# Graph layer on one core: the edge stage rebuilt around a broadcast row of relative targets, with W2 applied at the end

## What is computed

```python
h = maximum(layernorm(x), 0)
e = concatenate([h[src], h[dst]], axis=1)          # 200000 x 128
m = relu(e @ W1 + b1) @ W2 + b2                    # 200000 x 64
s = segment_sum(m, dst); cnt = segment_sum(1, dst)
out = x + s / maximum(cnt, 1)[:, None]
```

## Time and profile before

| what | value |
|---|---|
| median of 3 runs without a profile | 2057.42 us |
| profiled execution: first to last instruction | 3104.2 us |
| busy in it: PE / DVE / ACT / POOL | 1916.4 / 866.9 / 884.8 / 1516.6 us |
| indirect DMAs, mean busy of one | 1563, 944 ns |
| HBM traffic | 149 MB, 48 GB/s over the profiled span |
| mean granted TensorE clock | 0.748 |

### The profile page before, as it was taken

One profiled execution on the slowest core, in us unless ns is written; L12 is line 12 of the kernel. 1 busy time (PEld: TensorE's weight loads), 2 busy tenths in 40 slices (PEclk: granted clock), 3 DMA queues, 4 the chain that ended last, 5 costly groups with the idle time before them and its releaser, 6 DMA issues.

```text
span 3104.2 us, 46493 instructions
## 1 busy us (share of the span) xinstructions
PE 1916.4 (62%) x11540; PEld 1632.1 (53%) x11541; DVE 866.9 (28%) x2889; ACT 884.8 (29%) x2458; POOL 1516.6 (49%) x1611
## 2 busy tenths in 40 slices
PE   6256555655655566765556665565655667665568
PEld 6255444545555555554445555454555556554457
DVE  6122222222222222222222222222222222222224
ACT  3123222322222222222222222222222222222224
POOL 5445444544545444454445444454545445454451
PEclk9577777777777776677777667777777766677778
DMA  6311111111111111111111111111111111111111
GB/s 183 92 52 46 43 44 43 43 43 44 44 43 45 43 43 43 44 45 43 44 43 46 43 44 43 43 45 44 44 44 44 44 43 44 44 44 44 44 44 43
DMA packets 112927, 150.93 MB, mean 49 GB/s; under 512 B 32653, under 2 KB 83212, under 8 KB 112750
## 3 DMA queue, kind: packets, MB, share of 16 engines
q0 software_dynamic: 50016, 102.53, 12.6%
q1 hardware_dynamic: 62170, 46.62, 5.1%
q10 hardware_dynamic: 564, 0.23, 0.0%
HBM read 133.09 MB, written 16.07 MB: 48 GB/s over the span
## 4 chain that ended last, share of the span: by engine, by line
another core or an unknown queue 41%; PE 28%; issue 14%; ACT 10%; DVE 4%; DVEq 2%; DMA 1%; ACTq 1%; SPq 0%; POOL 0%; PEldq 0%; POOLq 0%
PE bank L874 12%; PE bank L885 11%; ACT spread L490 4%; ACT member L514 3%; PE bank L894 2%; DVE z L685 2%; ACT spans_i L497 1%; DVEq L689 1%; PE bank L975 1%; PE bank L817 1%; ACT idx L484 1%; PE bank L905 1%; PE bank L899 0%; PE bank L906 0%
## 5 line engine op out<-in xcount | busy, mean ns | idle before, releaser
L388 POOL DMA_INDIRECT g<-p_table,idx x1563 | 1476.0, 944 | 1504.6 <-ACT idx L484 1022.8
L874 PE MATMUL bank<-qw,spread 128*128 128x128 f32 x3126 | 647.1, 371 | 1044.4 <-ACT spread L490 985.2
L874 PEld LDWEIGHTS bank<-qw,spread 128*128 128x128 f32 x3126 | 551.4, 265 | 1106.8 <-ACT spread L490 857.0
L490 ACT CAST spread<-bank 128x512 f32<-128x512 bf16 x391 | 228.7, 585 | 1713.2 <-remote 1335.2
L885 PE MATMUL bank<-member,r 128*128 128x128 f32 x3126 | 616.9, 360 | 63.3 <-DVE acc L704 42.5
L697 DVE TENSOR_TENSOR area<-area,spans_i 1x128 f32 x391 | 109.6, 280 | 1949.0 <-ACT spans_i L497 1773.9
L885 PEld LDWEIGHTS bank<-member,r 128*128 128x128 f32 x3126 | 544.8, 263 | 106.6 <-DVE acc L704 38.9
L675 DVE TENSOR_SCALAR member<-columns,rel_e 128x128 f32<-128x128 f32 x1563 | 349.2, 290 | 107.0 <-PE bank L885 85.2
L508 ACT ACTIVATE r<-z 128x512 f32<-128x512 f32 x391 | 246.1, 630 | 371.5 <-DVE z L685 279.5
L685 DVE TENSOR_TENSOR z<-bank,g 128x512 f32<-128x512 f32 x391 | 263.7, 674 | 0.0
L514 ACT CAST member<-member 128x512 bf16<-128x512 f32 x391 | 235.3, 602 | 4.3 <-DVE member L675 4.3
(11 more groups left out here) (66 smaller groups left out, 434.8 us busy)
## 6 DMA issues: line engine op xcount, KB each, us to landing
qw<-q_table SPq DMA_DIRECT2D x391, 64.0 KB
g<-p_table,idx POOLq DMA_INDIRECT x1563
p_table<-area SPq DMA_DIRECT2D x10, 560.0 KB
q_table<-area SPq DMA_DIRECT2D x10, 560.0 KB
xs<-in_x_dram SPq DMA_DIRECT2D x5, 560.0 KB
out_dram<-xs SPq DMA_DIRECT2D x3, 672.0 KB
acc<-in_src_dram SPq DMA_DIRECT2D x1, 768.0 KB
acc<-in_dst_dram SPq DMA_DIRECT2D x1, 768.0 KB
```

The costliest lines, as they stand in the source:

```text
L388: nc.gpsimd.indirect_dma_start(out=g[:, k, j * HID:(j + 1) * HID], out_offset=None, in_=p_table, in_offset=bass.IndirectOffsetOnAxis(ap=id ...
L490: nc.scalar.copy(spread[:, k % 2, :, :].rearrange("p c e -> p (c e)")[:, 0:w], t_bank[k % 2][:, 0:w]).then_inc(spread_done, 1)
L874: last = nc.tensor.matmul(z_bank[k % 2][:, HID * j:HID * (j + 1)], spread[:, k % 2, j, :], qw[:, k, :], start=True, stop=True)
```

## The change

What it does, engine by engine:
- **W2 at the end.** `acc` holds sums of the 128 hidden values. The two multiplies per quad (lines 905, 906) and the copies before them go. At the end each of the 100 transposes becomes two fp32 matmuls into 64 columns: `acc` (125 strided columns as weights) by W2, and `count` (one partition, 125 strided columns as weights) by b2.
- **Spread.** At the start VectorE makes `rel_q` (bf16, four instructions of 128 x 512). Per quad TensorE broadcasts one row of it to 128 partitions (one bf16 matmul of 512 columns) and VectorE compares it with the partition's number, from PSUM, into `spread`. The transposes, the bf16 copy of member and the copy of spread go.
- **Member** is one instruction of 128 x 512 for a quad in place of four of 128 x 128, with two tensor inputs in SBUF. The counts read its upper halves as bf16.
- **Sum and relu in place** in the slot of the gather; a slot is free after the sum, in a ring of 16 instead of 12. Windows of q have a ring of 8.
- **GpSimd** gathers with indices straight from `src_e`, the first 16 quads without a wait of the edge stage. All engines' loops are unrolled, with waits on constants.
- ScalarE keeps one instruction per quad, the relu.

```diff
-RING = 12
+RING = 16
+WINDOWS = 8
@@ gpsimd
-            def gather(n, k, use):
-                ready = pool.to_reg(n + 1)
-                pool.wait_ge(p_out[0], all_out[0])
-                pool.wait_ge(idx_ready, ready)
+            pool.wait_ge(src_table, QT)
+            def gather(n):
+                k = n % RING
+                if n >= RING:
+                    pool.wait_ge(u_psum, n - RING + 1)
                 for j in range(chunks_of(n)):
                     nc.gpsimd.indirect_dma_start(
...
@@ scalar
+                for n in range(QUADS):
+                    w = HID * chunks_of(n)
+                    act.wait_ge(z_done, n + 1)
+                    nc.scalar.activation(g[0:ROWS, n % RING, 0:w], g[0:ROWS, n % RING, 0:w], ACT.Relu)\
+                        .then_inc(r_done, 1)
@@ vector
+            def rows_of():
+                dve.wait_ge(low_done, 1)
+                for t in range(QT):
+                    nc.vector.tensor_scalar(rel_q[:, t, :], dst_f[:, t, :], low[:, t:t + 1], FAR,
+                                            ALU.subtract, ALU.min).then_inc(row_table, 1)
...
+            def spread_of(n):
+                w = ROWS * chunks_of(n)
+                dve.wait_ge(row_done, n + 1)
+                if n >= 2:
+                    dve.wait_ge(zq_done, n - 1)
+                nc.vector.tensor_scalar(spread[:, n % 2, 0:w], row_bank[n % 2][:, 0:w], rows_f[:, :], None,
+                                        ALU.is_equal).then_inc(spread_done, 1)
+            def members_of(n):
+                if n >= MEMBERS:
+                    dve.wait_ge(u_psum, n - MEMBERS + 1)
+                nc.vector.tensor_tensor(member[0:ROWS, n % MEMBERS, :, :],
+                                        columns[0:ROWS, :].unsqueeze(1).to_broadcast([ROWS, 4, WIN]),
+                                        rel_e[0:ROWS, 4 * n:4 * n + 4].unsqueeze(2).to_broadcast([ROWS, 4, WIN]),
+                                        ALU.is_equal).then_inc(member_done, 1)
+            def add_rows(n):
+                w = HID * chunks_of(n)
+                rows_n = g[0:ROWS, n % RING, 0:w]
+                dve.wait_ge(zq_done, n + 1)
+                dve.wait_ge(gathered[n % RING], n // RING * 64 + 16 * chunks_of(n))
+                nc.vector.tensor_tensor(rows_n, z_bank[n % 2][0:ROWS, 0:w], rows_n, ALU.add).then_inc(z_done, 1)
+            def add_sums(n):
...
+                dve.wait_ge(u_psum, n + 1)
...
+                nc.vector.tensor_tensor(v, v, u_bank[n % 2][:, 0:WIN], ALU.add).then_inc(v_done, 1)
...
+                nc.vector.tensor_tensor(c, c, u_bank[n % 2][0:1, WIN:2 * WIN], ALU.add).then_inc(c_done, 1)
...
+                for n in range(QUADS + 2):
+                    if n + 1 < QUADS:
+                        spread_of(n + 1)
+                    if n < QUADS:
+                        add_rows(n)
+                    if n + 1 < QUADS:
+                        members_of(n + 1)
+                    if n >= 2:
+                        add_sums(n - 2)
+                scales()
@@ tensor
+            def broadcast_rows(n):
+                w = ROWS * chunks_of(n)
+                if n >= 2:
+                    pe.wait_ge(spread_done, n - 1)
+                nc.tensor.matmul(row_bank[n % 2][:, 0:w], ident16[:, n % 128:n % 128 + 1].to_broadcast([128, 128]),
+                                 rel_q[:, n // 128, 0:w], start=True, stop=True).then_inc(row_done, 1)
...
+            def sum_rows(to, rows_n, k, chunks):
                 for c in range(chunks):
+                    nc.tensor.matmul(to[0:1, WIN:2 * WIN], ones16[0:ROWS, :], ones_and_zeros(k, c),
+                                     start=c == 0, stop=c == chunks - 1)
+                for c in range(chunks):
+                    last = nc.tensor.matmul(to[:, 0:WIN], rows_n[:, HID * c:HID * (c + 1)], member[0:ROWS, k, c, :],
+                                            start=c == 0, stop=c == chunks - 1)
+                return last
...
+                broadcast_rows(0)
+                for n in range(QUADS + 1):
+                    if n + 1 < QUADS:
+                        broadcast_rows(n + 1)
+                    if n < QUADS:
+                        spread_q(n)
+                    if n >= 1:
+                        sum_edges(n - 1)
...
                     node = slice(BT * b + t, BT * b + t + (NP - 1) * NT + 1, NT)
-                    last = nc.tensor.transpose(bank[b % 8][0:NP, 128 * t:128 * (t + 1)], acc[:, node], ident[:, :])
+                    to = bank[b % 8][0:NP, 128 * t:128 * t + FEAT]
+                    nc.tensor.matmul(to, acc[:, node], w2[:, :], start=True, stop=False)
+                    last = nc.tensor.matmul(to, count[:, node], b2_row[:, :], start=False, stop=True)
```

More of the change, by code:

```diff
@@ L197, in columns_of, with chunk, ones_and_zeros @@
         def columns_of(table, t):
-            return table[:, QE * t:QE * (t + 1)].rearrange("e (q c) -> e c q", c=4)
+            return table[0:ROWS, 512 * t:512 * (t + 1)].rearrange("e (q c) -> e c q", c=4)
         def tile_of(b):
-            return b[:, :].rearrange("e (c q) -> e c q", c=4)
+            return b[0:ROWS, :].rearrange("e (c q) -> e c q", c=4)
+        def chunk(of, k, c):
+            return of[:, k, ROWS * c:ROWS * (c + 1)]
+        def ones_and_zeros(k, c):
+            return member[0:ROWS, k, c, :].bitcast(BF16).rearrange("e (w h) -> e w h", h=2)[:, :, 1]
         def parts(rows):
             return [(m, 4 * m, min(4, rows - 4 * m)) for m in range(-(-rows // 4))]
[L207 to L215, removed]
         def chunks_of(n):
-            return CHUNKS - 4 * n if isinstance(n, int) and n == QUADS - 1 else 4
+            return CHUNKS - 4 * n if n == QUADS - 1 else 4
         def if_one_window(eng, fast, general):
@@ L392, in general, with fast @@
+                        .then_inc(gathered[k], 16)
+            def fast():
+                for n in range(RING, QUADS):
+                    gather(n)
             def general():
                 first_rows_in(pool)
-                def gather_general(n):
-                    ready = pool.to_reg(n + 1)
-                    pool.wait_ge(p_out[0], all_out[0])
-                    pool.wait_ge(rows_ready, ready)
+                for n in range(QUADS):
+                    pool.wait_ge(rows_used, n + 1)
@@ L408, in _ @@
+                            .then_inc(rows_in, 16)
             for n in range(RING):
-                gather(n, n, 0)
-            if_one_window(pool, lambda: rounds(pool, RING, QUADS, gather), general)
+                gather(n)
+            if_one_window(pool, fast, general)
             for m, b in enumerate(SHARED):
@@ new lines, in spread_q @@
+            def spread_q(n):
+                pe.wait_ge(spread_done, n + 1)
+                pe.wait_ge(window_in[n % WINDOWS], 16 * (n // WINDOWS + 1))
+                if n >= 2:
+                    pe.wait_ge(z_done, n - 1)
+                for c in range(chunks_of(n)):
+                    last = nc.tensor.matmul(z_bank[n % 2][0:ROWS, HID * c:HID * (c + 1)], chunk(spread, n % 2, c),
+                                            qw[:, n % WINDOWS, :], start=True, stop=True)
+                last.then_inc(zq_done, 1)
```

343 lines of the change are left out of this document (89 added, 254 removed).

## The result

| what | before | after |
|---|---|---|
| median, lowest to highest | 2058.02 us (2057.03 to 2059.72, 4 runs) | 2184.7 us (2181.52 to 2188.78, 4 runs) |
| ratio after / before | | 1.0616 (95% interval 1.0601 to 1.0632) |
| profiled execution's span | 3104.2 us | 2184.9 us |
| first and last gather start | 62.0, 3023.7 us | 64.45, 2042.68 us |
| end part on TensorE, from the start of its first pass to the start of its last | 100 passes, 22.8 us | 400 passes, 128.9 us |

The changed kernel is slower by 126.7 us, 6.2%. The forecast was 2117 us, in a range of 2050 to 2138: the direction was right, the size was not.

A forecast was written before the change was run, and what follows sets the result against it. The prediction took GpSimd's nearly unbroken stream of gathers as the bound, plus what stands before and behind it. From 2057.4 us, -4 for gaps, -4.9 for hand-over and +68.8 for the end part gave 2117.3 us, range 2050 to 2138.

The forecast's parts named there:

- The bound: Whole kernel: GpSimd issues 1563 gathers nearly without pause from 62 us on, 1.248 us each, 1950.6 us.
- unnamed waits: ScalarE's 189 profiled waits, 1335.2 us, for something the profile cannot name; claimed absent in runs without a profile.
- Start: Before the first gather: changed memsets, index fill and relative rows cost zero; 2.7 us if their cover were gone.
- The stream: Gathers of the edge stage: shorter issue gaps give -4 us, the middle of bounds 0 and -8.7.
- the row of line 697: Edge stage: a gather beginning inside this two-SBUF-input instruction takes 0.95 us as any other, so compares hold no gather.
- third rival: Edge stage: the one-op member compare holds gathers, up to 262 us, at the middle 131, total 2248; chance 0.07.
- Hand-over: Behind the last gather: 8.9 us from last add to first TensorE pass falls to 4.0, taking 4.9 us off.
- End part: TensorE's end: 100 slots of four strided passes at 0.23 us, 92 us less 23.2 for the transposes, +68.8.
- low bound: End part: if the stride costs nothing, passes take 0.11 us, 44 us in all, +20.8.
- Unrolled streams, ring of 16: Edge stage: ring gives nothing where no wait is; rival that unrolled streams starve TensorE, some 2200 us, chance 0.03.
- five times as fast as needed: TensorE's instruction supply: straight-line code kept 20 passes at 0.11 us, ample for some 45 instructions in 4.99 us.
- The sum: Whole kernel: 2057.4 - 4 - 4.9 + 68.8 = 2117.3 us.

The follow-up runs named there:

- the paired one: Changed kernel with the count's product ahead of acc's in every second end slot; 2536.83 us on a chip with pauses, ratio 0.8177 to the kernel before.
- the kernel with both repairs: Changed kernel with the count's weights zero-padded to 125 partitions and the member compare's columns read from PSUM; 2119.93 us, ratio 1.0303 to the kernel before.

## Why the prediction was wrong

Two of its steps failed. It priced every pass of the end part by the transposes of before, which have one kind of weights, and so put the change between `acc` and `count` at nothing: 37 us. And it concluded from one row that a compare with two SBUF inputs holds no gather: 27.6 us. The two together are 65 of the 67 us by which it missed.

- **The bound**: right. GpSimd's stream runs without a wait from 64 us to its end. Right to take the unnamed waits out of the sum; wrong in saying that they cannot be there without a profile. Had the kernels been timed on the other kind of chip, the verdict would be the reverse: there the changed kernel takes about 2555 us by an estimate (the paired one's 2536.8 + 18.6) against 3107. A likely reason, not tested, is that ScalarE's copies, which feed GpSimd's indices in the earlier trace rows, are out of the gathers' way.
- **Start**: nothing forecast. The first gather started at 62.0 to 62.2 us in three profiles of before, and at 62.2 to 65.9 in those of kernels made from after: up to 4 us later, some 2 us in the middle.
- **The stream**: -4 us forecast, for shorter gaps, and nothing for a hold; the hold alone measured +27.6. The step that failed is the sentence that the row of line 697 speaks against the third rival. The gather in that row starts 0.22 us into an instruction of 0.28 us, so there was hardly anything left to be held by. The same trace has others. Timeline of before:

```profile
2063.51 0.28 DVE L697 TENSOR_TENSOR area<-area,spans_i 1x128 f32 x1 [2.75 <-ACT spans_i L497]
2063.60 1.02 POOL L388 DMA_INDIRECT g<-p_table,idx  x1 [0.30 <-issue]
```

In the three traces of before, gathers that start up to 0.1 us into line 697 take 1.00 us in the mean (6 of them), from 0.1 to 0.2 us 0.98 (27), later 0.945 (51); inside line 704, as long but with one input in PSUM, all 20 take 0.94 or 0.95. So one partition is enough, and the effect of the third rival stood in the record, small because the instruction is short. The rival was right that two SBUF inputs hold gathers (that it is their reading of the indices that waits isn't shown); its price is 27.6 us in place of the middle 131.

Why so little shows when the gathers of after that start inside line 599 (369, nearly all thirds of their quad) are sorted by how far in they start: from 0.1 to 0.2 us in they take 1.35 us (15 of them), from 0.2 to 0.3 us 1.26 (9), from 0.3 to 0.4 us 1.14 (12), from 0.4 to 0.5 us 1.03 (125), from 0.5 to 0.6 us 0.96 (179), later 0.94 (17). Each is held until about 0.1 us before the compare's end at 0.68. Of the 12 in the first 0.1 us, those within 0.03 us of the compare's start (7) take 0.94 and the others (5) 1.40 to 1.46. Gathers in whose course the compare starts take 0.944 (355): one already under way is not touched. Most start late in the compare, since VectorE's add waits for the landing of gathered rows and the compare follows it, so that the two keep step. So the price depends on the phase. On the chips with pauses that is another: 132 gathers of the paired kernel start 0.1 to 0.2 us in and take 1.32 us, one of them here:

```profile
1005.16 0.68 DVE L599 TENSOR_TENSOR member<-columns,rel_e 128x512 f32<-128x512 f32 x1
...
1005.35 1.31 POOL L375 DMA_INDIRECT g<-p_table,src_e  x1 [0.31 <-issue]
```

If each of the 391 lost as much, 0.38 us, it would be some 150 us in all: an estimate from this class. The Trainium skill (SBUF — State Buffer, Who interferes with whom) says that a VectorE instruction with two SBUF inputs contends with a GpSimd instruction that reads SBUF. The forecast went against it, and the runs agree with it: a third step of 1.318 us with two such inputs, 1.248 with one.
- **Hand-over**: 4.0 us forecast, 4.9 measured (2046.03 to 2050.89).
- **End part**: +68.8 forecast, 128.9 - 22.8 = +106.1 measured. The price of a strided pass, 0.23 us whatever the clock, was right for passes of one kind; missing was the change between weights on 128 partitions and on one, 200 times 0.19 = 37 us. The low bound was mis-sized as well: 0.11 us is the packed pass at the 2.4 GHz level, and the end part ran at 1.2, where it takes 0.213, so that even packed weights of one kind would have come to some 85 us and not 44. The trace of before had a hint of the change: in the stretch of the earlier trace rows, lines 905 and 906 alternate in just that way. Timeline of TensorE there, in the kernel before:

```profile
3035.42 0.49 PE L905 MATMUL bank<-w 128*128 128x128 f32 x2
...
3035.83 0.48 PE L906 MATMUL bank<-spans_i,b_row 1*128 1x128 f32 x2
...
3036.25 1.16 PE L874 MATMUL bank<-qw,spread 128*128 128x128 f32 x8
...
3037.67 1.16 PE L885 MATMUL bank<-member,r 128*128 128x128 f32 x8 [0.26 <-ACT r L508]
```

Two passes take 0.41 us there, packed, and eight of line 874 1.16: 0.2 a pass against under 0.15, both at a granted clock of 1.00. The forecast removed these lines and never asked what one of them costs.
- **Unrolled streams, ring of 16**: nobody starved, no slot was waited for. (The forecast's "five times as fast as needed" doesn't follow from its row: 45 instructions in 4.99 us are one every 0.11 us, and 20 passes with their 20 weight loads in 2.35 us one every 0.06, twice as fast.) The edge stage's lighter engines bought nothing, as nothing waited for them but on chips with pauses.
- **The sum**: 106.1 + 27.6 - 6.5 = 127.2, against the measured 126.7. The -6.5 are what the kernel with both repairs shows for hand-over and the rest: 2119.9 - 2057.7 = 62.2, less 91.5 - 22.8 = 68.7 for its end part. The forecast had -8.9 there: -4.9 for the hand-over and -4 for gaps. Taken apart, if the end of before is on this chip as in its profile: hand-over 4.9 - 8.9 = -4.0, start +2.6 (64.7 against 62.1), behind the last pass -0.4, which leaves -4.7 for the stream and its landing. That fits the -4 for gaps, but no trace of before without pauses shows them.

## What to carry to other kernels

Price an instruction by a row with its own operands, its own clock level, and the same kind of instruction just before it on its engine. Read a contention from all places where the two instructions meet, sorted by how far in the second one starts: one row from near the end of the first shows nothing. Don't alternate fp32 products with one-partition and full-height weights; pad the short one with zero rows, or at least put two of a kind side by side. And when VectorE works beside indirect DMAs of GpSimd, keep one of its two tensor inputs in PSUM.

## What the runs showed of the hardware

- A pair of products whose weights alternate between 128 partitions and one costs 1.29 us a slot against 0.92 (four fp32 passes, 125 strided columns, clock 0.50); with packed weights still 1.20. The weight loads themselves are no longer for it (0.31 us), but they no longer overlap. Why, is open.
- A strided fp32 weight load of 125 columns sets 0.229 us a pass, at a granted clock of 0.50 and of 0.93 alike, with 64 or 128 moving columns. A packed pass of 128 columns takes 0.111 us at 1.00 and 0.213 at 0.50, so that the stride costs half the time at one level and next to nothing at the other.
- TensorE's clock stayed at 0.50 through all 129 us of an end part in which it was never idle.
- A gather that starts while VectorE reads two SBUF inputs is held to near that instruction's end, on 128 partitions (0.94 to 1.35 us and more) and on one (to 1.03, in an instruction of 0.28 us); one already under way is not (0.944). With one of the inputs in PSUM it isn't held.
- Three of the five chips that the experiments ran on had pauses while indirect DMAs ran, and take 3107 us for a kernel that takes 2058 on the others. The cause is open.
